# A 16-head attention with its exponentials left in PSUM and its value rows masked by ScalarE

## The reference, cut to what matters

```python
def _L0_xattn_ref(queries, keys, values, Wq, bq, Wk, bk, Wv, bv, Wo, bo):
    # 16 heads of 8 features; first 32 keys of the context under the causal mask
    q = (queries @ Wq.T + bq).reshape(N, L, H, -1)
    k = (keys @ Wk.T + bk).reshape(N, S, H, -1)
    v = (values @ Wv.T + bv).reshape(N, S, H, -1)
    sm = jnp.einsum('nlhd,nshd->nlhs', q, k) / math.sqrt(D)
    sm = jnp.where(causal_mask[None, :, None, :], -jnp.inf, sm)
    sm = jax.nn.softmax(sm, axis=-1)
    attn = jnp.einsum('nlhs,nshd->nlhd', sm, v)
    return attn.reshape(N, L, H * D) @ Wo.T + bo
x = x + _L0_xattn_ref(_layernorm(x, axis=-1), ctx_1024, ctx_1024, ...)
...
x = x + _L3_attn_ref(_layernorm(x, axis=-1), ...)    # the same attention, q, k and v from x
```

## Time and profile before

| | |
|---|---|
| median of 3 runs | 3825.92 us |
| the profiled execution | 3828.19 us |
| its span | 3825.7 us |
| busy: TensorE, VectorE, ScalarE, GpSimd | 74%, 67%, 43%, 38% |
| mean granted clock of TensorE | 0.857 of full speed |
| tile loop of x0, of a3 | from 65 to 248 us, from 3405 to 3586 us |

### The profile page before, as it was taken

One profiled execution on the slowest core, in us unless ns is written; L12 is line 12 of the kernel. 1 busy time (PEld: TensorE's weight loads), 2 busy tenths in 40 slices (PEclk: granted clock), 3 DMA queues, 4 the chain that ended last, 5 costly groups with the idle time before them and its releaser, 6 DMA issues. The chain is left out here.

```text
span 3825.7 us, 102951 instructions
## 1 busy us (share of the span) xinstructions
PE 2837.8 (74%) x27568; PEld 2246.5 (59%) x27569; DVE 2580.4 (67%) x9045; ACT 1654.5 (43%) x5099; POOL 1453.3 (38%) x1363
## 2 busy tenths in 40 slices
PE   5872378659999788657999972248839999967662
PEld 3651377537777677534777751247727777746562
DVE  5977521268888845556888885662158888869635
ACT  1112034337777622224777765204317777711111
POOL 1520057525655400002555540007615555525252
PEclk9985589879999989878999995559969999979765
DMA  2000244511111000201232310204524444300122
GB/s 80 0 0 14 91 119 141 138 37 36 35 36 35 24 1 0 94 12 43 70 70 69 70 39 0 53 18 144 132 77 107 104 103 103 89 1 0 33 78 73
DMA packets 213222, 226.54 MB, mean 59 GB/s; under 512 B 31235, under 2 KB 180739, under 8 KB 212452
## 3 DMA queue, kind: packets, MB, share of 16 engines
q1 hardware_dynamic: 200452, 199.44, 19.6%
q0 software_dynamic: 12672, 25.98, 2.6%
HBM read 202.77 MB, written 22.55 MB: 59 GB/s over the span
## 5 line engine op out<-in xcount | busy, mean ns | idle before, releaser
L1656 POOL TENSOR_TENSOR sx<-sx,rs 128x1028 f32<-128x1028 f32 x384 | 732.1, 1906 | 589.8 <-DVE rs L1787 589.8
L1735 ACT ACTIVATE sx<-sx,nm 128x257 f32<-128x257 f32 x1536 | 770.7, 505 | 349.1 <-DVE nm L1781 349.1
L1781 DVE CUSTOM_DVE_ANT_0 sx<-bank,rows 128x257 f32<-128x257 f32 x1024 | 394.0, 422 | 78.7 <-PE bank L1725 73.7
L1408 ACT ACTIVATE hT<-bank,B 128x128 f32<-128x128 f32 x714 | 206.1, 368 | 324.6 <-PE bank L1376 322.8
L1735 ACT ACTIVATION_READ_ACCUMULATOR sx<-sx,nm 128x1 f32 x1536 | 290.5, 189 | 0.0
L1725 PE MATMUL bank<-kT,qb 32*128 32x257 f32 x3072 | 276.0, 428 | 3.6 <-DVE nm L1781 3.6
L1797 DVE COPY pt<-bank 128x512 f32<-128x512 f32 x384 | 263.3, 686 | 4.6 <-PE bank L1676 4.6
L1676 PE MATMUL bank<-C,sx 128*128 128x128 f32 x1536 | 251.9, 286 | 3.4 <-DVE a L1830 3.4
L1434 DVE TENSOR_TENSOR yb<-bank,b2s 128x128 f32<-128x128 f32 x159 | 46.3, 291 | 302.1 <-PE bank L1389 298.2
L1714 PE MATMUL bank<-pt,vs 128*32 128x128 f32 x6144 | 247.4, 279 | 0.0
L1688 PE MATMUL bank<-ct,W 128*128 128x257 f32 x768 | 234.8, 388 | 17.0 <-DVEq L1768 15.5
(11 more groups left out here) (385 smaller groups left out, 6337.0 us busy)
## 6 DMA issues: line engine op xcount, KB each, us to landing
ct<-in_ctxT SPq DMA_DIRECT2D x384, 128.5 KB
W<-in_L_w SPq DMA_DIRECT2D x159, 256.0 KB
rows<-rows_x SPq DMA_DIRECT2D x256, 128.5 KB
keep<-rows_keep SPq DMA_DIRECT2D x128, 128.5 KB
yg<-copy_outs SPq DMA_DIRECT2D x40, 256.0 KB
token_rows<-XN SPq DMA_DIRECT2D x24, 256.0 KB, 2.3
vl<-last_v SPq DMA_DIRECT2D x384, 2.0 KB
W<-in_L_w SPq DMA_DIRECT2D x39, 128.0 KB
```

What stands on the lines that cost most here:

```text
L1656: pool.tensor_tensor(sx[:, j, :, 0:KEYS], sx[:, j, :, 0:KEYS], rs[:, j, :].unsqueeze(2).to_broadcast([P, 4, KEYS]), ALU.mult).then_inc(p_r ...
L1735: ins = act.activation(sx[:, j, h, 0:KEYS], sx[:, j, h, 0:KEYS], ACT.Exp, bias=nm[:, j, h:h + 1], scale=-1.0, accum_out=sm[:, j, h:h + 1])
L1781: dve.tensor_tensor_reduce(sx[:, j, h, 0:KEYS], B[h][:, 0:KEYS], add, -1.0, 3.0e38, ALU.add, ALU.min, nm[:, j, h:h + 1]).then_inc(s_summed ...
```

## The change

Four things change in the tile loop, all in `attn16`:

1. The scores of tile t go to bank SB[t % 4] out of four (banks 0, 1, 6, 7). The subtraction, the exponential and the reads of sum and product work on that bank; only the product is written to SBUF (e). The scores of tile t now wait for the product of tile t-4 (`e_normed`).
2. The eviction of the value rows moves from VectorE to ScalarE, as four activations of 128 columns with a pointer scale (the head's 0/1 column) and a pointer bias (bvh, bias times that column, made once). They stand behind the next tile's exponential.
3. The transpose of the values reads VT directly, without the copy, and is issued a tile earlier, together with the addition to X (now of tile t-3), between subtraction and sum.
4. The loops are written out for all 32 tiles, with no registers and no branch.

```diff
+                SB = [B[0], B[1], B[6], B[7]]
+                bvh = sb2("bvh", [P, 4])
...
-                    for t in range(2):
-                        stages(t, t % 2, lambda x: 0 <= x < N)
-                    lp = steps.loop(1, N // 2, per) if steps else eng.Fori(1, N // 2)
-                    with lp as i:
-                        for q in range(2):
-                            stages(i * 2 + q, q, lambda x: True)
-                    for t in range(N, N + depth):
+                    for t in range(N + depth):
                         stages(t, t % 2, lambda x: 0 <= x < N)
...
-                            pe.wait_ge(*centred(t - 1))
+                            pe.wait_ge(*e_normed(t - 3))
...
-                                pe.matmul(B[q][:], ident, mask4x[:].rearrange("p b j k -> p (b j k)"), start=True,
+                                pe.matmul(SB[t % 4][:], ident, mask4x[:].rearrange("p b j k -> p (b j k)"), start=True,
...
-                        act.wait_ge(*centred(t + 1))
-                        act.activation(e[:, q, :], e[:, q, :], ACT.Exp).then_inc(exp_ready.sem, 1)
-                    run(act, stages, 0)
+                        if ok(t):
+                            act.wait_ge(*centred(t + 1))
+                            act.activation(SB[t % 4][:], SB[t % 4][:], ACT.Exp).then_inc(exp_ready.sem, 1)
+                        u, z = t - 1, 1 - q
+                        if ok(u):
+                            if u == 0:
+                                act.wait_ge(*b_done(1))
+                            act.wait_ge(*av_psum(u + 1))
+
+                            act.wait_ge(*y_psum(u - 1))
+                            for j in range(4):
+                                ins = act.activation(m[:, z, j, :], B[2 + z][:, j * P:(j + 1) * P], ACT.Identity,
+                                                     bias=bvh[:, j:j + 1], scale=const("head")[:, j:j + 1])
+                            ins.then_inc(heads_ready.sem, 1)
+                    run(act, stages, 1)
...
+                    dve.tensor_scalar(bvh[:], const("head"), v(bv), None, ALU.mult).then_inc(b_done.sem, 1)
+
+                    def turn(t, q):
+
+                        dve.wait_ge(*v_built(t - 1))
+                        dve.transpose(vt[:, q, :], VT[:, bass.ds(t * P, P)]).then_inc(v_turned.sem, 1)
...
+                            sv = SB[t % 4][:].rearrange("p (g k) -> p g k", k=S)
+                            st_.link(dve.tensor_reduce(mx[:, q, :], sv, AX.X, ALU.max))
+                            dve.tensor_tensor(sv, sv, mx[:, q, :].unsqueeze(2).to_broadcast([P, 16, S]),
                                               ALU.subtract).then_inc(centred.sem, 1)
-                        u, z = t - 1, 1 - q
-                        if ok(u):
-                            dve.wait_ge(*av_psum(u + 1))
-
-                            dve.wait_ge(*y_psum(u - 1))
-                            dve.scalar_tensor_tensor(out=m[:, z].rearrange("p j t -> p (j t)"), in0=B[2 + z][:],
-                                                     scalar=v(bv), in1=const("diag512"), op0=ALU.add,
-                                                     op1=ALU.mult).then_inc(heads_ready.sem, 1)
...
-                        u, z = t - 2, q
+                        u, z = t - 3, 1 - q
                         if ok(u):
                             dve.wait_ge(*y_psum(u + 1))
                             xt_ = X[:, bass.ds(u, 1), :]
                             dve.tensor_tensor(xt_, xt_, B[4 + z][:, 0:P].unsqueeze(1), ALU.add).then_inc(x_added.sem, 1)
-                    run(dve, stages, 2, st_, 10)
+                        if ok(t + 1):
+                            turn(t + 1, 1 - q)
+                        if ok(t):
+                            dve.wait_ge(*exp_ready(t + 1))
+                            sv = SB[t % 4][:].rearrange("p (g k) -> p g k", k=S)
+                            st_.link(dve.tensor_reduce(sm[:, q, :], sv, AX.X, ALU.add))
+                            st_.link(dve.reciprocal(sm[:, q, :], sm[:, q, :]))
+                            dve.tensor_tensor(e[:, q, :].rearrange("p (g k) -> p g k", k=S), sv,
+                                              sm[:, q, :].unsqueeze(2).to_broadcast([P, 16, S]), ALU.mult).then_inc(e_normed.sem, 1)
+                            dve.wait_ge(*e_normed(t + 1))
+                            dve.wait_ge(*av_psum(t - 1))
+                            dve.transpose(pt[:, q, :], e[:, q, :]).then_inc(pT_ready.sem, 1)
+                    run(dve, stages, 3)
```

More of the change, by code:

```diff
@@ L370, in attn16 @@
                 heads_ready, y_psum, x_added = sig("heads_ready", 32), sig("y_psum", 32), sig("x_added", 32)
-                copied = sig("copied", 1)
+                copied, b_done, e_normed = sig("copied", 1), sig("b_done", 1), sig("e_done", 32)
+                SB = [B[0], B[1], B[6], B[7]]
+                bvh = sb2("bvh", [P, 4])
                 N = TILES
@@ L379, in attn16, with run @@
                 block = c2.enter_context(nc.Block())
-                def run(eng, stages, depth, steps=None, per=0):
-                    for t in range(2):
-                        stages(t, t % 2, lambda x: 0 <= x < N)
-                    lp = steps.loop(1, N // 2, per) if steps else eng.Fori(1, N // 2)
-                    with lp as i:
-                        for q in range(2):
-                            stages(i * 2 + q, q, lambda x: True)
-                    for t in range(N, N + depth):
+                def run(eng, stages, depth):
+                    for t in range(N + depth):
                         stages(t, t % 2, lambda x: 0 <= x < N)
@@ L412, in stages @@
                             pe.wait_ge(*q_built(t + 1))
-                            pe.wait_ge(*centred(t - 1))
-                            if isinstance(t, int) and t == 0:
+                            pe.wait_ge(*e_normed(t - 3))
+                            if t == 0:
                                 pe.wait_ge(*copied(1))
                             if causal:
-                                pe.matmul(B[q][:], ident, mask4x[:].rearrange("p b j k -> p (b j k)"), start=True,
+                                pe.matmul(SB[t % 4][:], ident, mask4x[:].rearrange("p b j k -> p (b j k)"), start=True,
                                           stop=False, skip_group_check=True)
                             for b in range(BPT):
-                                ins = pe.matmul(B[q][:, b * P:(b + 1) * P], qb[:, q, b].rearrange("p j s -> p (j s)"),
+                                ins = pe.matmul(SB[t % 4][:, b * P:(b + 1) * P], qb[:, q, b].rearrange("p j s -> p (j s)"),
                                                 kb[:, q, b].rearrange("p j s -> p (j s)"), start=not causal, stop=True,
@@ L459, in _ @@
                     ins.then_inc(copied.sem, 1)
+                    dve.tensor_scalar(bvh[:], const("head"), v(bv), None, ALU.mult).then_inc(b_done.sem, 1)
+                    def turn(t, q):
+                        dve.wait_ge(*v_built(t - 1))
+                        dve.transpose(vt[:, q, :], VT[:, bass.ds(t * P, P)]).then_inc(v_turned.sem, 1)
                     def stages(t, q, ok):
                         if ok(t):
-                            dve.wait_ge(*v_built(t - 1))
-                            tok = bass.ds(t * P, P)
@@ L466, in stages @@
-                            st_.link(dve.tensor_copy(vt[:, q, :], VT[:, tok]))
-                            dve.transpose(vt[:, q, :], vt[:, q, :]).then_inc(v_turned.sem, 1)
+                            if t == 0:
+                                turn(t, q)
                             dve.wait_ge(*scores(t + 1))
[L469 to L472, removed]
+                            sv = SB[t % 4][:].rearrange("p (g k) -> p g k", k=S)
@@ L482, in stages @@
[L482 to L490, removed]
```

## The result

The changed kernel takes 3781.79 us, the median of 4 runs (3778.86 to 3782.61), against 3827.58 us for the kernel before on the same chip. The ratio is 0.9878, 95% interval [0.9861, 0.9895]: 46 us faster. The forecast was 3780, 46.2 us less. The profiled span is 3777.1 us.

A forecast was written before the change was run, and what follows sets the result against it. VectorE's queue was taken to set the pace. At 4.53 us a tile in x0 and 4.41 in a3, plus 2.0 per stage, 22.7 and 23.7 are saved, less 0.2: 46.2 us, so 3780 us, range 3768 to 3796.

The forecast's parts named there:

- VectorE's chain: VectorE's tile, maximum to X addition, counted through the wait for the exponential: 4.44 us, 4.41 with an exponential of 0.60.
- slow start: Start of x0 and a3: at the low granted clock TensorE sets the pace, estimated to cost 2.0 us per stage.
- new idle time: VectorE before the sum: the remaining fill of 1.10 us leaves 0.29 us waiting for the exponential.
- the move to PSUM: Scores and exponentials in PSUM: exponential 0.60 instead of 0.63; VectorE's instructions no different in x0, 0.69 in a3.
- GpSimd: the turn comes a stage earlier, no cost: GpSimd's 3.1 us per tile: values are turned a stage earlier, so kb is there sooner, at no cost.
- loop of two tiles: x0, TensorE's 4.51 us plus VectorE's 4.49: 9.00 over two tiles, 4.50 each, taken as 4.53; a3's loop gives 4.0.
- Four banks: TensorE's scores: its order is unchanged, so four banks let it run no further ahead.
- second rival: TensorE keeps x0 back further through waits of 0.2 us each: 4.85 a tile, time 3790; chance 0.06.
- Four evictions: ScalarE, behind the next tile's exponential: 1.5 to 2.9 us per tile, covered under 4.4.
- third rival: Written-out loops need instruction fetches: 39 packets stopping the chain 2.0 us each add 78 us, 3858; chance 0.05.
- the late maximum: VectorE in x0 before: 0.44 us from value transpose to the next maximum, within the tile's sum of 5.30.
- Ends: After the last transpose: the last evictions are ready before TensorE is free, so nothing is lost.

The follow-up runs named there:

- e5_exp_sbuf: The changed kernel with the exponentials back in SBUF, where subtraction, exponential, sum and product work on e; ratio 0.9967 to the kernel before.
- e3_two_banks: The changed kernel with two score banks in turn instead of four, scores waiting for the product of tile t-2; 3780.19 us, ratio 0.9864.
- e1_unroll_only: The kernel before with only its tile loops written out for all 32 tiles; 3826.85 us against 3830.71, ratio 0.9984.
- e2_rolled: The changed kernel in loops of four tiles with registers, and the copy of the values back ahead of their transpose; 3781.75 us, ratio 0.987.
- e7_evict_twice: The changed kernel with ScalarE's four evictions issued twice, first into a spare buffer nobody reads; ratio 0.9864 to the kernel before.
- e11_after_light_pool: The changed kernel with GpSimd's three masked products cut to a quarter of their columns from the third tile on; ratio 0.9847 to the kernel before.
- e10_sbuf_light_pool: The changed kernel with exponentials in SBUF and GpSimd's masked products cut to a quarter from the third tile; ratio 0.9872 to the kernel before.

## Why the prediction was right

**VectorE's chain.** Booking the chain over the exponential, and not the 0.95 us of instructions that went, was the step that made the forecast. Worked out at 4.41 us, plus 2.0 for the slow start over 31 tiles, 4.47; measured 4.48 in a3, and 4.41 in its later tiles. The new idle time, 0.29 us by an exponential of 0.63, is 0.24, as the exponential takes 0.58, under the 0.60 that I chose too. Moving the eviction was worth 0.34 of its 0.74 in a3, as the chain says: most of the rest had covered the exponential.

**What I did not see.** The prediction priced the move to PSUM at 0.03 us a tile and would have passed the change without it as nearly as good. It would have been 34 us worse (e5_exp_sbuf). I had read the 0.74 of the product in a3 and called it a form, where it was a first sign of the meeting with GpSimd: kb ended at 3498.9 and the product began at 3498.71. The forecast came out right because the change had both parts; the step "GpSimd: the turn comes a stage earlier, no cost" was right only because of the other, and that was luck.

**TensorE and the loop of two tiles.** 4.53 us plus the slow start, 4.59; measured 4.56. The two tiles read take 9.02 us, worked out at 9.00, and without the mask x0 falls to 4.48 and its later tiles to 4.41. Four banks do nothing here, as the prediction said and e3_two_banks shows. The second rival falls, since x0 stands far below 4.85.

**ScalarE.** Four evictions take 1.50 us, the low end of 1.5 to 2.9, and the place behind the exponential is right: in front of it they cost 1.2 us a tile.

**Written-out loops.** No fetch stopped the chain; the third rival falls, although the instruction queue carried 52 packets after against 39 before:

```profile
q8 instruction: 52, 0.85, 0.1%
```

I booked the loop itself at nothing. Written out alone it is worth 6 us (e1_unroll_only), about a seventh of the gain. My chain held this without naming it: it takes the tile that I read, in which the product takes 0.69 us and stands 0.73 before the transpose, and leaves out the stretch between the addition to X and the next maximum. That I took the late maximum in it for VectorE's own time was a misreading; the scores came late.

**The slow start.** The 2.0 us for each stage were right in size, 1.8 in x0 and 2.2 in a3, and right in kind: one wait of VectorE for the scores while TensorE ran slowly. My check of the term was not. It took 5.30 us for every x0 tile of before, where every other one takes 5.22, so x0 lost some 2 us at its start and not 0.8. And in the traces of e2_rolled in both stages, of e7_evict_twice in x0 and of e11_after_light_pool in a3 the wait is missing, so this term could have come out at nothing.

**Ends.** x0's tail is about as long as before. a3's is 3.3 us shorter, which I had not forecast: its last output matmuls ran at 1.16 us for eight records where they took 2.08. The rows of before and after:

```profile
3583.87 2.08 PE L440 MATMUL bank<-W,m 128*128 128x128 f32 x8
...
3585.98 0.29 DVE L495 TENSOR_TENSOR X<-X,bank 128x128 f32<-128x128 f32 x1 [2.44 <-PE bank L440]
```

```profile
3534.55 0.97 PEld L436 LDWEIGHTS bank<-W,m 128*128 128x128 f32 x8
3534.55 1.16 PE L436 MATMUL bank<-W,m 128*128 128x128 f32 x8
...
3535.75 0.29 DVE L489 TENSOR_TENSOR X<-X,bank 128x128 f32<-128x128 f32 x1 [1.38 <-PE bank L436]
```

The granted clock over the ends is 0.54 before (3577 to 3587) and 1.00 after (3530 to 3536). With the small costs against it (bvh takes 0.22 us each time and not 0.1), this is why 47.2 us in the loops and 3 us at the end became 48.6 us in the span; the remaining stages differ by a microsecond or two. The higher clock there does not come with the change alone: in e3_two_banks the last output matmuls take 1.16 us too, in e2_rolled and e10_sbuf_light_pool 2.08 as before. What sets it is not shown. Without these 3.3 us the time would have come out some 3 us higher, still inside the range; that it fell within 2 us of the forecast is in part luck.

## What to carry to other kernels

When an instruction leaves the engine that sets the pace, look for what it had covered: what is won is the chain that remains, here 0.34 us of 0.74, and the next gain lies in filling the gap (one more tile in flight gave 31 us more). An engine that is busy less than half the time still must do its work in the right order: the same evictions in front of the exponential made the kernel slower than before. Read more than one tile, and the first ones by themselves: a mean over a stage hides one wait of 2 us, which is as much as several of the effects sought here. And before pulling work forward, see what will then run at the same time: a VectorE product with both inputs in SBUF and GpSimd's products held each other up, and leaving one input in PSUM avoided it.

## What the runs showed of the hardware

Unexpected was the size of that collision and how it looks: product 1.38 us instead of 0.69 and GpSimd's product 1.49 instead of 1.04, with no idle time before either, so the lists of waits do not show it. The duration of one form compared between two kernels does. An exponential of 512 columns took 0.58 us from PSUM to PSUM and 0.63 from SBUF to SBUF; an activation of 128 columns with pointer scale and pointer bias out of PSUM took 0.46, four in a row 1.50. A rolled loop cost VectorE 0.08 us between product and transpose (0.81 against 0.73, e2_rolled, tiles inside and outside the loop), and in the kernel before 0.06 between the addition to X and the copy in every other x0 tile (0.23 against 0.17 written out).
